# Attention weights turned by VectorE and DMA instead of TensorE, on one Trainium2 core

## Chip, core and metric

One core of a Trainium2 chip runs the kernel. The metric is the device time of one execution in microseconds (us). The kernel before took 1949.81 us, the median of 3 runs (1949.67 to 1951.08).

## What is computed

128 graphs of 128 nodes, width 512, 16 heads of 32, all in float32. `spatial_encoding` and `edge_encoding` are both `adj`, so the bias is `2 * adj`.

```python
q, k, v = (split_heads(x @ W.T) for W in (Wq, Wk, Wv))
a = einsum('bhnd,bhmd->bhnm', q, k) * 512 ** -0.5 + (adj + adj)[:, None]
row_nonzero = any(a != 0, axis=-1, keepdims=True)
p = softmax(where(row_nonzero, a, -inf)); p = where(isnan(p), 0, p)
o = einsum('bhnm,bhmd->bhnd', p, v)
out = layernorm(x + merge_heads(o) @ Wo.T)
```

## The kernel before, in words

Four graphs make a group (`GG`), 32 groups in all. Four heads make a tile, four tiles a group. One **round** `f` (the code says phase) handles one tile of one group: 4 graphs x 4 heads = 16 score blocks of 128 x 128. There are 128 rounds, `LAST` is the last. Every engine has its own instruction list, written out by hand, and the lists meet in semaphores.

Matrix products of weights (kinds k, q, v, o) are made as three float32r products of high and low parts, 12 matmuls of 512 columns a product, 16 products a group. `PLAN` deals them to the rounds: (kind, index, groups ahead). They go through three PSUM banks `ps_w` in turn, and `wait_bank` waits until the product three uses ago has been taken out of its bank.

A round on the engines:

- **PE** (`build`, tensor block): `turn(f-1, i)` transposes the 16 blocks of normalised weights of the round before (L468) into `ps_w` and `ps_o`; `scores(f)` (L481); `values(f-1)` (L495), which multiplies v by the turned weights `e_t` into `ps_o`; then the products of `slots(f)` (L396 to L407).
- **ACT**: takes products out of their banks (`take`, L573), copies turned weights from PSUM to `e_t` (`turned_out`), runs 16 exps with row sums (`exps`, L630) once `bias` has made the rows of a graph, writes the high part of the values (`values_hi`), normalises output rows (`normalise`, L616), and splits x chunks (`chunk_hi`).
- **DVE**: `add` (L757) and `moments` (L768, L770) for output rows, `bias` (L781, 16 instructions: minus scores minus doubled adj, with row minimum), `any_nonzero` (L791: maximum of 2048 elements a lane, so that with the minimum a row of zeros is found), `abs_largest` (L800, L805), and for each half (two graphs) `reciprocals` (L813) and `normalise` (L822 and L826, two instructions of 512 elements); `values_lo` (L719); `double_adj` (L729) once a group.
- **POOL**: low parts of x chunks (`chunk_lo`, L301) and the small operations of layernorm (`ln`, L324 to L339).
- **SP**: all loads and stores, by group.

`neg_a` (biased rows), `e_sb` (weights) and `e_t` (turned weights) each exist once: `bias(f)` waits for all exps of round f-1, and DVE runs `normalise` of the second half before the next `bias`.

Of the kernel before, what the change touches and what calls it, by code (L numbers as in the profile page):

```python
# [6 lines left out]
F32R = mybir.dt.float32r  # L7
ALU = mybir.AluOpType
# [12 lines left out]
GG = 4  # L21
# [3 lines left out]
BANKS = 3  # L25
SCALE = float(D) ** -0.5
# [9 lines left out]
PLAN = [[("k", 1, 0), ("q", 1, 0), ("v", 0, 1), ("v", 1, 1)],  # L36
# [3 lines left out]
FIRST_PLAN = [[("q", 1, 0), ("v", 0, 0), ("v", 1, 0), ("v", 2, 0), ("v", 3, 0)],  # L40
# [3 lines left out]
LAST_PLAN = [[("k", 1, 0), ("q", 1, 0), ("k", 2, 0)],  # L44
             [("q", 2, 0), ("k", 3, 0), ("o", 0, -1)],
             [("q", 3, 0), ("o", 1, -1)],
             [("o", 2, -1), ("o", 3, -1)]]
BEFORE = [("k", 0, 0), ("q", 0, 0), ("k", 1, 0)]
LAST = PHASES - 1
# [3 lines left out]
def slots(f):  # L53

    g, t = f // TILES, f % TILES
    if f < 0:
        plan, g = BEFORE, 0
    elif f == PHASES:
        plan = AFTER
    elif g == GROUPS - 1:  # L60
        plan = LAST_PLAN[t]
    else:
        plan = PLAN[t] if g else FIRST_PLAN[t]
    return [(kind, g + ahead, index) for kind, index, ahead in plan]
# [6 lines left out]
def bank_uses():  # L71

    uses = list(slots(-1))
    for f in range(PHASES):
        if f:
            uses += [("t", f - 1, i) for i in range(0 if f == LAST else 1, GG)]
        uses += slots(f)
    return uses + [use for use in slots(PHASES) if use[2] != 1]  # L80
# [10 lines left out]
def window_chunk(f):  # L91

    g, t = f // TILES, f % TILES
    chunk = {3: (g + 2, 1), 0: (g + 1, 3)}.get(t)
    return chunk if chunk and 2 <= chunk[0] < GROUPS and f < PHASES else None


def late_chunk(f):
    g, t = f // TILES, f % TILES
    chunk = {2: (g + 2, 0), 3: (g + 2, 2)}.get(t)  # L100
    return chunk if chunk and 2 <= chunk[0] < GROUPS and f < PHASES else None


def build(nc, xt_d, x_d, adj_d, wq_d, wk_d, wv_d, wo_d, out_d):
    ctx = ExitStack()
    with ctx:
# [6 lines left out]
        def sem(name):  # L113
# [14 lines left out]
        e_t = sb("e_t", [P, GG, TH, NODES])  # L128
# [6 lines left out]
        neg_min = sb("neg_min", [P, GG, TH])  # L135
        sums = sb("sums", [P, GG, TH])
        recip = sb("recip", [P, GG, TH])
        abs_max = sb("abs_max", [P, GG, TH])
# [12 lines left out]

        ps_w = [bank(f"ps_w{n}") for n in range(BANKS)]
# [11 lines left out]
        x_loaded = sem("x_loaded")  # L164
# [11 lines left out]
        biased = sem("biased")  # L176
        min_done = sem("min_done")
        exp_done = sem("exp_done")
        turned = sem("turned")
        turned_copied = sem("turned_copied")  # L180
        values_done = sem("values_done")
        abs_done = sem("abs_done")
# [12 lines left out]
        stored = sem("stored")  # L195
# [3 lines left out]
        xt_stage = {(g, c): buffer[:, c].rearrange("p a b -> p (a b)")  # L199
                    for g, buffer in ((0, neg_a), (1, e_t)) for c in range(CH)}  # L200
# [8 lines left out]
        def turned_bank(f, i):  # L209
            if f == LAST:  # L210
                return ps_s[(1, 2, 3, 1)[i]]
            return ps_w[USE["t", f, i] % BANKS] if ("t", f, i) in USE else ps_o
# [7 lines left out]
        def _(sp):  # L220
# [7 lines left out]
            def load_chunk(g, c):  # L228
                if g >= GROUPS:
                    return  # L230
                if g > 2 or c >= 2:
# [5 lines left out]
            def store(g, i):  # L237
                if g >= 0:
                    sp.wait_ge(normed, count("o", g, i))
                    sp.dma_start(out_d[g, :, i, :], x_row(g, i)).then_inc(stored, 16)  # L240

            def load_x(g):
                if g == 0:
                    sp.wait_ge(w_hi_done, 4 * CH)
                    sp.wait_ge(wo_lo_done, CH)
                else:
                    sp.wait_ge(stored, 16 * GG * g)
                sp.dma_start(x_sb[:, :, :], x_d[g]).then_inc(x_loaded, 16)
# [13 lines left out]
            for g in range(GROUPS):  # L262
                store(g - 2, 3)
                if g + 1 < GROUPS:
                    if g:
                        sp.wait_ge(biased, GG * TILES * g)
                    sp.dma_start(adj_sb[:, (g + 1) % PAIR], adj_d[g + 1]).then_inc(adj_loaded[(g + 1) % PAIR], 16)
                if g:
                    load_x(g - 1)
                load_chunk(g + 2, 0)  # L270
                load_chunk(g + 2, 1)
                if g == GROUPS - 1:
                    sp.wait_ge(values_done, GG * g)
                    sp.dma_start(v_sb[:, 1 - g % PAIR], x_d[g]).then_inc(last_x_loaded, 16)
                store(g - 1, 0)
                store(g - 1, 1)
                load_chunk(g + 2, 2)
                store(g - 1, 2)
                load_chunk(g + 2, 3)
            store(GROUPS - 2, 3)  # L280
            for i in range(GG):
                store(GROUPS - 1, i)
            sp.wait_ge(stored, 16 * GRAPHS)

        @block.gpsimd
        def _(pool):
# [13 lines left out]
            def rest(out, whole, hi):  # L300
                return pool.tensor_tensor(out, whole, hi.bitcast(F32), ALU.subtract)  # L301

# [76 lines left out]
            for f in range(PHASES):  # L379
# [544 lines left out]
```

## Time and profile before

| | |
|---|---|
| median of 3 runs | 1949.81 us |
| the profiled execution | 1949.59 us, its span 1947.8 us |
| TensorE busy | 1928.2 us (99%) |
| VectorE, ScalarE, GpSimd busy | 1475.5, 1490.9, 419.5 us |
| DMA | 116.41 MB, 60 GB/s |
| granted TensorE clock | 0.998 of full speed |

Busy time counts an engine's own instructions. It doesn't say what the engine would have had to wait for; that is read from the start times of a round in the timeline. The full clock is 2.4 GHz.

### The profile page before, as it was taken

The numbers are of one execution on the slowest core, as the hardware profiler recorded it, in microseconds if no ns is written. First come the engines' busy times: TensorE is split into PE (matmuls) and PEld (weight loads), VectorE is DVE, ScalarE is ACT, GpSimd is POOL, SyncE is SP. The second block draws the span as 40 slices with busy tenths as digits, with TensorE's granted clock in tenths as the row PEclk, the third lists the DMA queues.
The fourth block names the chain that finished last, engine by engine and source line by source line (L and its number), as shares of the span: only waits on it lengthen the run. The fifth ranks groups of instructions, "written<-read, shape, count | busy, mean of one in ns | idle before, by whom it ended". The sixth has DMA issues, their size and how long they took to land. (4 is left out here: it accounts for less than half of the span.)

```text
span 1947.8 us, 49249 instructions
## 1 busy us (share of the span) xinstructions
PE 1928.2 (99%) x16402; PEld 1607.4 (83%) x16402; DVE 1475.5 (76%) x6068; ACT 1490.9 (77%) x5394; POOL 419.5 (22%) x1268
## 2 busy tenths in 40 slices
PE   9999999999999999999999999999999999999997
PEld 7888888888888888888888888888888888888885
DVE  6787777778777887778777777877788777877776
ACT  7787778777777777788777877777777777877775
POOL 2122111222112221222211122211222122221102
PEclk9999999999999999999999999999999999999999
DMA  4121111211112201122111221112220112211111
GB/s 152 50 72 39 51 61 66 71 55 40 56 66 72 72 29 55 61 72 72 36 54 61 66 71 55 40 55 66 72 72 28 55 61 71 72 35 54 50 61 45
DMA packets 48637, 116.41 MB, mean 60 GB/s; under 512 B 5376, under 2 KB 5376, under 8 KB 44288
## 3 DMA queue, kind: packets, MB, share of 16 engines
q1 hardware_dynamic: 47808, 112.22, 17.0%
q8 instruction: 131, 2.15, 0.5%
q14 instruction: 122, 1.00, 0.2%
q10 hardware_dynamic: 576, 1.05, 0.2%
HBM read 79.69 MB, written 33.55 MB: 58 GB/s over the span
## 5 line engine op out<-in xcount | busy, mean ns | idle before, releaser
L630 ACT ACTIVATE e_sb<-neg_a,neg_max 128x128 f32<-128x128 f32 x2048 | 792.3, 391 | 93.5 <-DVE neg_max L781 93.2
L781 DVE CUSTOM_DVE_ANT_0 neg_a<-ps_s,adj_sb 128x128 f32<-128x128 f32 x2048 | 442.6, 286 | 369.1 <-PE ps_s L481 369.1
L404 PE MATMUL ps_w<-xt_hi,w_lo 128*128 128x512 f32 x1020 | 412.5, 404 | 0.0
L405 PE MATMUL ps_w<-xt_lo,w_hi 128*128 128x512 f32 x1020 | 398.4, 391 | 0.0
L630 ACT ACTIVATION_READ_ACCUMULATOR e_sb<-neg_a,neg_max 128x1 f32 x2048 | 388.1, 190 | 0.0
L826 DVE SCALAR_TENSOR_TENSOR e_sb<-e_sb,r_inv 128x512 f32<-128x512 f32 x512 | 331.0, 687 | 9.2 <-DVE r_inv L822 0.5
L791 DVE TENSOR_REDUCE neg_min<-neg_a 128x16 f32<-128x2048 f32 x129 | 292.7, 2269 | 4.4
L301 POOL TENSOR_TENSOR xt_lo<-xt_raw,xt_hi 128x512 fp32r<-128x512 f32 x120 | 155.6, 1297 | 576.9 <-ACT xt_hi L573 576.9
L407 PE MATMUL ps_w<-xt_hi,w_hi 128*128 128x512 f32 x1020 | 273.8, 390 | 0.0
L404 PEld LDWEIGHTS ps_w<-xt_hi,w_lo 128*128 128x128 f32 x1020 | 191.2, 187 | 62.3 <-issue 25.6
L573 ACT ACTIVATE e_t<-ps_o 128x512 f32<-128x512 f32 x126 | 75.2, 597 | 201.4 <-PE ps_o L468 201.4
L407 PEld LDWEIGHTS ps_w<-xt_hi,w_hi 128*128 128x128 f32 x1020 | 191.5, 188 | 42.3
L405 PEld LDWEIGHTS ps_w<-xt_lo,w_hi 128*128 128x128 f32 x1020 | 191.5, 188 | 36.4
L324 POOL TENSOR_TENSOR ln_tmp<-mean_var,constants 128x1 f32<-128x1 f32 x122 | 23.1, 190 | 858.8 <-DVE mean_var L770 854.1
L573 ACT ACTIVATE e_t<-ps_w 128x512 f32<-128x512 f32 x382 | 200.5, 606 | 1.4 <-PE ps_w L468 1.2
L404 PE MATMUL ps_w<-w_hi,xt_lo 128*128 128x512 f32 x512 | 199.2, 389 | 0.0
L405 PE MATMUL ps_w<-w_lo,xt_hi 128*128 128x512 f32 x512 | 199.2, 389 | 0.0
L404 PE MATMUL ps_w<-w_hi,o_lo 128*128 128x512 f32 x496 | 193.1, 389 | 0.0
L405 PE MATMUL ps_w<-w_lo,o_hi 128*128 128x512 f32 x496 | 193.0, 389 | 0.0
L468 PE MATMUL ps_w<-ident,e_sb 128*128 128x128 f32 x1528 | 188.1, 273 | 1.7 <-DVE e_sb L826 1.7
L573 ACT ACTIVATE v_sb<-ps_w 128x512 f32<-128x512 f32 x128 | 76.3, 596 | 137.0 <-PE ps_w L407 136.7
L468 PEld LDWEIGHTS ps_w<-ident,e_sb 128*128 128x128 f32 x1528 | 170.6, 140 | 2.4 <-issue 2.4
(105 smaller groups left out, 2838.9 us busy)
## 6 DMA issues: line engine op xcount, KB each, us to landing
x_sb<-x SPq DMA_DIRECT2D x31, 1024.0 KB, 4.8
out<-x_sb SPq DMA_DIRECT2D x124, 256.0 KB, 2.4
xt_raw<-xt SPq DMA_DIRECT2D x120, 256.0 KB, 2.8
adj_sb<-adj SPq DMA_DIRECT2D x32, 256.0 KB, 2.9
v_sb<-wk ACTq DMA_DIRECT2D x4, 256.0 KB, 6.3
neg_a<-xt SPq DMA_DIRECT2D x4, 256.0 KB, 5.8
e_sb<-wq SPq DMA_DIRECT2D x4, 256.0 KB, 7.7
v_sb<-wv SPq DMA_DIRECT2D x4, 256.0 KB, 8.3
```

The lines of the kernel that those rows point to most:

```text
L301: return pool.tensor_tensor(out, whole, hi.bitcast(F32), ALU.subtract)
L324: pool.tensor_tensor(ve, mean_var[:, i, 1:2], eps, ALU.add).then_inc(pool_step, 1)
L404: pe.matmul(out, lhs_lo(c), rhs_hi(c), start=(c == 0), stop=False)
L405: pe.matmul(out, lhs_hi(c), rhs_lo(c), start=False, stop=False)
L407: last = pe.matmul(out, lhs_hi(c), rhs_hi(c), start=False, stop=(c == chunks - 1))
L468: last = pe.transpose(turned_bank(f, i)[:, h * P:(h + 1) * P], e_sb[:, i, h, :], ident[:, :])
L573: return act.activation(out, in_, ACT.Copy, scale=scale)
L630: last = act.activation(e_sb[:, i, h, :], neg_a[:, i, h, :], ACT.Exp, scale=-1.0, bias=neg_max[:, i, h:h + 1], accum_out=sums[:, i, h:h + 1])
L781: last = dve.tensor_tensor_reduce(out=neg_a[:, i, h, :], in0=ps_s[h][:, i * NODES:(i + 1) * NODES], in1=adj_sb[:, g % PAIR, i, :], scale=- ...
L791: dve.tensor_reduce(neg_min[:, a:b].rearrange("p a b -> p (a b)"), neg_a[:, a:b].rearrange("p a b c -> p (a b) c"), AX.X, ALU.max).then_in ...
L826: dve.scalar_tensor_tensor(out=e_sb[:, i], in0=e_sb[:, i], scalar=BIG, in1=r_inv[:, i].unsqueeze(2).to_broadcast([P, TH, NODES]), op0=ALU. ...
```

## The change

- PE turns weights in the last round alone. In the others DVE transposes the 32 x 32 blocks of a half in one instruction (`turn_blocks`, from `e_sb` to a new buffer `e_b`), SP saves each half to DRAM (`save_blocks`, rows of 1 KB) and, once both are saved, loads them back with four DMAs, one for each 32 partitions, which puts the blocks in their places in `e_t` (`move_blocks`, rows of 2 KB).
- Values are made two rounds later than their scores: PE's round is `values(f-2)`, `scores(f)`, products.
- `PLAN` gives each round one k, one q, one v and one o product.
- `any_nonzero` no longer reads 2048 elements on DVE. POOL compares the biased rows of a half with zero into bytes, folds them as 32-bit integers three times (`zeros`), and DVE adds up the 16 bytes a row that are left and compares the sum with 128.
- `normalise` of a half is one instruction of 1024 elements. `bias` also waits until POOL has read the rows before.
- x rows are loaded by 256 KB instead of 1 MB; SP's list goes by rounds.
- `add` stands ahead of `bias`, `moments` and `values_lo` behind it; POOL's layernorm stands behind the zeros.

```diff
-PLAN = [[("k", 1, 0), ("q", 1, 0), ("v", 0, 1), ("v", 1, 1)],
-        [("k", 2, 0), ("q", 2, 0), ("o", 0, -1), ("o", 1, -1)],
-        [("k", 3, 0), ("q", 3, 0), ("o", 2, -1), ("o", 3, -1)],
-        [("k", 0, 1), ("q", 0, 1), ("v", 2, 1), ("v", 3, 1)]]
+PLAN = [[("k", 1, 0), ("q", 1, 0), ("v", 3, 0), ("o", 3, -2)],
+        [("k", 2, 0), ("q", 2, 0), ("v", 0, 1), ("o", 0, -1)],
+        [("k", 3, 0), ("q", 3, 0), ("v", 1, 1), ("o", 1, -1)],
+        [("k", 0, 1), ("q", 0, 1), ("v", 2, 1), ("o", 2, -1)]]
...
+            def save_blocks(f, half):
+                sp.wait_ge(transposed, 2 * f + half + 1)
+                sp.dma_start(blocks_d[f % 2, :, :, half], blocks_half[:, half]
+                             ).then_inc(saved[half], 16)
+
+            def move_blocks(f):
+
+                for half in range(2):
+                    sp.wait_ge(saved[half], 16 * (f + 1))
+                if f:
+                    sp.wait_ge(values_done, f)
                 else:
...
+                for b in range(BLOCKS):
+                    rows = slice(BLOCK * b, BLOCK * (b + 1))
+                    sp.dma_start(e_t[rows, :].rearrange("p (a c) -> p a c", a=BLOCKS),
+                                 blocks_d[f % 2, :, b].rearrange("(a j) m c -> j a (m c)", a=BLOCKS)
+                                 ).then_inc(moved, 16)
...
+            for f in range(PHASES):
+                g, t = f // TILES, f % TILES
+                if f:
+                    save_blocks(f - 1, 1)
+                store(f - O_LAG - 2)
+                load_x(f - GG)
+                load_chunk(loaded_chunk(f))
...
+                if f:
+                    move_blocks(f - 1)
...
+                if f < LAST:
+                    save_blocks(f, 0)
...
+            def zeros(f, half):
+
+
+                n = 2 * f + half
+                rows = neg_a[:, 2 * half:2 * half + 2].rearrange("p i h n -> p (i h n)")
+                pool.wait_ge(biased, GG * f + 2 * half + 2)
+                if n:
+                    pool.wait_ge(folded_done, n)
+                pool.tensor_scalar(is_zero[:, :].bitcast(U8), rows, 0.0, None, ALU.is_equal).then_inc(zero_step, 1)
+                words = is_zero[:, :].rearrange("p (r c) -> p r c", r=2 * TH)
+                pool.wait_ge(zero_step, 3 * n + 1)
+                pool.tensor_tensor(folded_once[:, :, :], words[:, :, 0:16], words[:, :, 16:32], ALU.add).then_inc(zero_step, 1)
...
             for f in range(PHASES):
+                chunk_lo(window_chunk(f))
+                zeros(f, 0)
+                zeros(f, 1)
                 if f:
                     ln(f - 1, -1)
...
+                if f:
                     pe.wait_ge(o_lo_done, f)
+                if f < LAST:
+                    pe.wait_ge(moved, 16 * BLOCKS * (f + 1))
...
             for f in range(LAST):
-                if f:
-                    for i in range(GG):
-                        turn(f - 1, i)
+                if f > 1:
+                    values(f - 2, range(GG), ps_o)
                 scores(f)
-                if f:
-                    values(f - 1, range(GG), ps_o)
...
+            def turn_blocks(f, half):
+                if f:
+                    dve.wait_ge(saved[half], 16 * f)
+                dve.wait_ge(normalised, 2 * f + half + 1)
+                dve.transpose(blocks[:, half],
+                              e_sb[:, 2 * half:2 * half + 2].rearrange("p i h (b j) -> p (i h) b j", b=BLOCKS)
+                              ).then_inc(transposed, 1)
...
+            for f in range(PHASES):
                 if f:
                     add(f - 1, -1)
+                bias(f)
+                if f:
                     moments(f - 1, -1)
-                if f % TILES == TILES - 1 and f + 1 < PHASES:
+                if f > 1:
+                    values_lo(f - 2)
+                if f % TILES == TILES - 1 and f < LAST:
                     double_adj(f // TILES + 1)
...
+                for half in range(2):
+                    any_nonzero(f, half)
+                    reciprocals(f, half)
+                    normalise(f, half)
+                    if f < LAST:
+                        turn_blocks(f, half)
+                    else:
+                        add(LAST, half)
```

## Rows read from the trace of the kernel before

**Rows 1.** The page, part 1: busy time, share, instructions of each engine.

```profile
PE 1928.2 (99%) x16402; PEld 1607.4 (83%) x16402; DVE 1475.5 (76%) x6068; ACT 1490.9 (77%) x5394; POOL 419.5 (22%) x1268
```

**Rows 2.** Timeline of PE, one round: start, duration, engine, line, operation.

```profile
929.09 0.60 PE L468 MATMUL ps_o<-ident,e_sb 128*128 128x128 f32 x4
...
930.92 1.17 PE L481 MATMUL ps_s<-k_sb,q_sb 32*128 32x128 f32 x32
932.03 1.08 PE L495 MATMUL ps_o<-e_t,v_sb 128*32 128x128 f32 x32
933.04 0.50 PE L404 MATMUL ps_w<-xt_hi,w_lo 128*128 128x512 f32 x1
...
944.07 0.60 PE L468 MATMUL ps_o<-ident,e_sb 128*128 128x128 f32 x4
```

**Rows 3.** Timeline of PE: the scores of rounds 4 and 124.

```profile
76.70 1.17 PE L481 MATMUL ps_s<-k_sb,q_sb 32*128 32x128 f32 x32
...
1875.08 1.17 PE L481 MATMUL ps_s<-k_sb,q_sb 32*128 32x128 f32 x32
```

**Rows 4.** Timeline of DVE, one round from its first bias.

```profile
932.16 0.29 DVE L781 CUSTOM_DVE_ANT_0 neg_a<-ps_s,adj_sb 128x128 f32<-128x128 f32 x1 [4.71 <-PE ps_s L481]
...
935.66 2.29 DVE L791 TENSOR_REDUCE neg_min<-neg_a 128x16 f32<-128x2048 f32 x1
...
938.05 0.18 DVE L800 SCALAR_TENSOR_TENSOR abs_max<-neg_max,neg_min 128x16 f32<-128x16 f32 x1
...
940.06 0.20 DVE L813 RECIPROCAL recip<-sums 128x8 f32<-128x8 f32 x1
...
941.76 0.68 DVE L719 TENSOR_TENSOR o_lo<-ps_o,o_hi 128x512 fp32r<-128x512 f32 x1
942.36 0.68 DVE L757 TENSOR_TENSOR x_sb<-ps_w,x_sb 128x512 f32<-128x512 f32 x1
943.07 0.70 DVE L768 BATCH_NORM_STATS2 ln_stats<-x_sb 128x6 f32<-128x512 f32 x1
943.80 0.18 DVE L770 BATCH_NORM_AGGREGATE mean_var<-ln_stats 128x2 f32<-128x6 f32 x1
```

**Rows 5.** Groups by form: shapes, count, busy us, mean ns, idle before.

```profile
L791 DVE TENSOR_REDUCE neg_min<-neg_a 128x16 f32<-128x2048 f32 x127 | 290.3, 2286 | 4.4
...
L791 DVE TENSOR_REDUCE neg_min<-neg_a 128x8 f32<-128x1024 f32 x2 | 2.4, 1209 | 0.0
```

**Rows 6.** Timeline of ACT: first and last of the 16 exps of that round.

```profile
933.19 0.40 ACT L630 ACTIVATE e_sb<-neg_a,neg_max 128x128 f32<-128x128 f32 x1 [1.35 <-DVE neg_max L781]
...
939.46 0.40 ACT L630 ACTIVATE e_sb<-neg_a,neg_max 128x128 f32<-128x128 f32 x1
```

**Rows 7.** Groups by form, POOL.

```profile
L301 POOL TENSOR_TENSOR xt_lo<-xt_raw,xt_hi 128x512 fp32r<-128x512 f32 x120 | 155.6, 1297 | 576.9 <-ACT xt_hi L573 576.9
...
L327 POOL TENSOR_TENSOR ln_tmp<-ln_tmp,constants 128x1 f32<-128x1 f32 x122 | 67.2, 551 | 0.0
...
L329 POOL TENSOR_TENSOR ln_tmp<-ln_tmp 128x1 f32<-128x1 f32 x122 | 23.6, 193 | 9.6
...
L296 POOL TENSOR_SCALAR_AFFINE_SELECT ident<-ident 128x128 f32<-128x128 f32 x1 | 0.3, 292 | 0.2 <-POOL two_constants L294 0.2
```

**Rows 8.** Timeline of DVE and POOL at 960.8.

```profile
960.81 0.39 DVE L729 TENSOR_SCALAR adj_sb<-adj_sb 128x512 f32<-128x512 f32 x1
960.84 0.41 POOL L335 TENSOR_TENSOR ln_tmp<-ln_tmp,constants 128x1 f32<-128x1 f32 x1
```

**Rows 9.** The page, parts 3 and 6: DMA queue, and us to landing.

```profile
q1 hardware_dynamic: 47808, 112.22, 17.0%
...
x_sb<-x SPq DMA_DIRECT2D x31, 1024.0 KB, 4.8
out<-x_sb SPq DMA_DIRECT2D x124, 256.0 KB, 2.4
```

**Rows 10.** Timeline of POOL: the four operations that split wo.

```profile
31.59 5.00 POOL L301 TENSOR_TENSOR w_lo<-x_sb,w_hi 128x512 fp32r<-128x512 f32 x4 [9.40 <-ACT w_hi L573]
```

More of the change, by code:

```diff
@@ L25 @@
 BANKS = 3
+BLOCK = 32
+BLOCKS = NODES // BLOCK
 SCALE = float(D) ** -0.5
@@ L63, in slots @@
         plan = PLAN[t] if g else FIRST_PLAN[t]
-    return [(kind, g + ahead, index) for kind, index, ahead in plan]
+    return [(kind, g + ahead, index) for kind, index, ahead in plan if g + ahead >= 0]
 def count(kind, g, index):
@@ L163, in build @@
         xt_loaded = [sem(f"xt_loaded{n}") for n in range(2)]
-        x_loaded = sem("x_loaded")
+        x_loaded = [sem(f"x_loaded{i}") for i in range(GG)]
         last_x_loaded = sem("last_x_loaded")
@@ L176, in build @@
         biased = sem("biased")
+        zero_step = sem("zero_step")
+        folded_done = sem("folded_done")
         min_done = sem("min_done")
         exp_done = sem("exp_done")
+        transposed = sem("transposed")
+        saved = [sem(f"saved{half}") for half in range(2)]
+        moved = sem("moved")
         turned = sem("turned")
@@ L668, in _ @@
             take(-1, 2)
-            for f in range(LAST):
-                n = len(slots(f))
-                if f:
-                    take(f - 1, -1)
-                    for i in range(GG):
-                        turned_out(f - 1, i)
-                    normalise(f - 1, -2)
+            for f in range(PHASES):
+                if f > 1:
+                    values_hi(f - 2)
                 chunk_hi(window_chunk(f))
@@ L680, in _ @@
                     exps(f, i)
[L681 to L688 removed]
+                    if i % 2:
+                        take(f, i // 2)
+                if f == 0:
+                    weight_hi("o")
+                else:
                     normalise(f - 1, -1)
                 chunk_hi(late_chunk(f))
[L691 to L700 removed]
+                for s in range(2, len(slots(f))):
+                    take(f, s)
             values_hi(LAST - 1)
[L702 to L705 removed]
+            turned_out(0)
+            turned_out(1)
             values_hi_half(0)
[L707 to L708 removed]
+            turned_out(2)
+            turned_out(3)
             values_hi_half(1)
[L710 removed]
             normalise(LAST, 0)
@@ L813, in reciprocals, with normalise @@
                 dve.reciprocal(recip[:, two], sums[:, two]).then_inc(recip_done, 1)
-            def normalise(f, half, nonzeros):
+            def normalise(f, half):
                 n = 2 * f + half
@@ L824, in normalise @@
                 dve.wait_ge(r_done, n + 1)
-                for i in range(2 * half, 2 * half + 2):
-                    dve.scalar_tensor_tensor(out=e_sb[:, i], in0=e_sb[:, i], scalar=BIG,
-                                             in1=r_inv[:, i].unsqueeze(2).to_broadcast([P, TH, NODES]),
-                                             op0=ALU.min, op1=ALU.mult).then_inc(normalised, 1)
+                dve.scalar_tensor_tensor(out=e_sb[:, two].rearrange("p i h n -> p (i h) n"),
+                                         in0=e_sb[:, two].rearrange("p i h n -> p (i h) n"), scalar=BIG,
+                                         in1=r_inv[:, two].rearrange("p i h -> p (i h)").unsqueeze(2
+                                         ).to_broadcast([P, 2 * TH, NODES]),
+                                         op0=ALU.min, op1=ALU.mult).then_inc(normalised, 1)
+            def turn_blocks(f, half):
+                if f:
+                    dve.wait_ge(saved[half], 16 * f)
[3 more added lines that the diff above has]
+                              ).then_inc(transposed, 1)
             for c in range(CH):
@@ L919 @@
     out = nc.dram_tensor("out", [GROUPS, NODES, GG, D], F32, kind="ExternalOutput").ap()
-    build(nc, *aps, out)
+    blocks = nc.dram_tensor("blocks", [2, P, BLOCKS, 2, 2 * TH * BLOCK], F32, kind="Internal").ap()
+    build(nc, *aps, out, blocks)
     r = run_bass_kernel_spmd(nc, [arrays], core_ids=[0])
```

309 lines of the change are left out of this document (121 added, 188 removed), and 4 rows, old and new, of the table FIRST_PLAN.

## The prediction

> **What bounds the kernel now.** I read the busy shares first: TensorE (PE) works 99% of the span [rows 1]. Next I laid one round of its timeline out by the start times of its four kinds of work [rows 2]: transposes 929.09 to 930.92, so 1.83 us; scores to 932.03, 1.11 us; values to 933.04, 1.01 us; the four weight products until the next transposes at 944.07, 11.03 us. The sum is 14.98 us and nothing in it is a wait. The starts of the scores of rounds 4 and 124 [rows 3] give (1875.08 - 76.70) / 120 = 14.99 us a round, so one round stands for all. The span of 1947.8 is then 76.7 before round 4, 1798.4 of rounds and 72.7 behind.
>
> **PE after the change.** The 16 transposes of a round go, in all rounds but the last: 13.15 us a round are left (1.01 + 1.11 + 11.03). The products are only dealt out differently, one of each kind to a round. That is the floor; the rest asks which engine or queue can't hold 13.15.
>
> **VectorE (DVE), term by term, start to start** [rows 4]. add 942.36 to 943.07: 0.71. bias 932.16 to 935.66: 3.50. moments: 0.73 and about 0.20. values_lo 941.76 to 942.36: 0.60. Doubling adj every fourth round: 0.10. These are 5.84 us. Each half then has a reduction of 128 bytes a lane, a compare, reciprocal, r_inv, normalise and the new transpose. Reciprocal to the end of normalise takes 940.06 to 941.76, 1.70, and the merged normalise costs the same. A tiny operation with a wait takes 0.28 (938.05 to the next). The byte reduction: the two reductions of rows 5 differ by 1.08 us for 1024 elements, which leaves about 0.27. The transpose of 1024 elements isn't in this trace. Its nearest row is the one-source reduction of 1024 elements, 1.209 us [rows 5], 1.15 in sequence. Below, the doubling of adj does 512 elements in 0.39 [rows 8], so 0.7 for 1024; above I allow half the reduction's pace, 2.2. I take 1.15: the row nearest in size, with one source and 4-byte elements. A half is 0.27 + 0.20 + 1.70 + 1.15 = 3.32 us, two are 6.65, and DVE needs 12.5 us a round. The removed reduction of 2048 elements (2.2 in sequence) pays for nearly all of the two transposes. So DVE has only 0.65 us to spare against PE.
>
> **ScalarE (ACT)** loses four copies and has 16 exps, from 933.19 with one copy between to the last at 939.46 [rows 6]: 6.7 us, with at most six other operations of 0.5 to 0.8. It fits in 13.15. In the chain it matters thus: bias starts at 0, the exps end at 7.7, and DVE reaches the second half at 5.1 + 3.3 = 8.4 anyway. Hidden, with 0.7 us of cover.
>
> **GpSimd (POOL)** gets per half a compare of 1024 elements and three folds of 128, 64 and 32 words. Its rows [rows 7]: a two-input operation takes 1.297 us at 512 elements and 0.193 at one, so 2.16 ns an element; the one-input select takes 0.292 at 128, so 0.8 to 1.5 ns an element, depending on how much of it is fixed. The folds by the two-input row: 0.47, 0.33, 0.26 and 0.3 of waits between, 1.4 us. The compare, P: 1.0 to 1.6 by the select, 2.4 by the two-input row. I take about 1.3, the one-input row being nearer in kind. A half costs 2.7. The first can start when two graphs are biased, 1.8, and is done at 4.5, before DVE asks at 5.1; the second at 7.2, before 8.4. POOL's whole round is 5.4 + 2.3 (layernorm) + 1.3 (a chunk) = 9.0 us. Hidden while P stays below about 1.6; the rival below says what lies above.
>
> A POOL operation of 0.19 us took 0.41 when it started 0.03 us behind DVE's doubling of adj, whose duration was unchanged [rows 8]: the later one waited. The Trainium skill (SBUF — State Buffer, Who interferes with whom) says that a DVE instruction with two SBUF inputs and a POOL instruction that reads SBUF exclude each other, whoever issued first. By that rule normalise may wait for a POOL fold, up to 0.47 a half; the rows allow nought to that. I charge 0.2 a half: DVE 12.9, still under 13.15. The skill's GPSIMD Engine Reference (4.1, Engine selection) calls one-input work on POOL roughly line-rate; an estimate by it would be P = 1.0 and the sum the same.
>
> **The queue of SyncE (SP) and DMA.** Each round adds two saves of 512 KB in 1 KB pieces and four moves of 256 KB in 2 KB pieces, six issues of about 0.4 us on SP, which has 13 us. Now q1 moves 112.22 MB in 17.0% of 16 engines [rows 9], 339 GB/s while busy. 2 MB more is 6.2 us of all engines a round, 7.5 if the short pieces cost half as much again; with today's 2.6 it is at most 10.1 of 13.15. Latency: 256 KB land in 2.4 us, 1 MB in 4.8 [rows 9]; a save about 3.2, then the moves at 4.8 plus 1.2 of issue, plus up to 2.3 behind the loads and stores that SP issues between: 9 to 12 us from the second transpose to the last move. Values wait for it. The second transpose ends 11.8 us after bias starts, and values of the next round but one begin 24.05 us after it: 12.2 us of cover. Saves wait for transposes and moves for saves, and behind them in SP's order stand the stores and x loads; those have a round to spare. What is late next, if the moves are: PE, by T = (14.15 + L) / 2, with L the latency.
>
> **Ends.** In round 0 the zeros stand on POOL behind the split of wo, 31.59 to 36.6 now [rows 10], some 3 us earlier after the change. Two halves of 2.7 end about 39, DVE's second half about 43, and bias of round 1 waits for it; today it isn't so. DVE and ACT then take some 11.2 us a round (no adds yet): bias of round 3 at 65, q of round 4 at 73, its scores at 74, against 76.70. All gain of the first rounds but 3 us is lost. At the end rounds 125 and 126 have three products and go by DVE's 12.5; the last values wait for a move, but turns remain on PE as now: 71 us against 72.7.
>
> **Sum.** 74 + 120 x 13.15 + 71 = 1723 us of span. The profiled execution took 1949.59 at a span of 1947.8, and the median is 1949.81, so 2 to 3 more: **1726 us**.
>
> **Rivals.**
> *A, the forecast: PE keeps the bound*, rounds of 13.1 to 13.3 us, 1715 to 1750. For it: all floors above lie below PE's. Against: three of them by less than 1 us. 45%.
> *B, POOL sets the pace through DVE.* If P is long, the compare of the second half is running when normalise of the first wants to start, and must end first: at 3.25 + 2P after bias. Then normalise, folds behind it, transpose, the second half and add make the round 10.0 + 2P. It decides from P = 1.6. At 2.0 it is 14.0 us and 1828 us. At 2.4, the two-input row, 14.8 and 1925. By the skill's rule of exclusion above, this is how it comes; without exclusion P = 2.4 makes the round only about 13.4 us (second half's zeros at 9.4, then 3.32 and 0.71). 26%, between 1750 and 1930.
> *C, the moves come late.* With L = 14 (the four moves get in each other's way, each filling only 32 partitions), T = 14.1 us, 1838 us. For it: it is the longest chain in the change and its row is an interpolation. 13%; 1750 to 1850.
> *D, the transpose goes at half pace*: DVE 12.5 + 2.1 = 14.6 us, 1900 us. Nothing in the trace speaks for it. 8%.
> *E, slower than before: B beyond its rows.* Place and mechanism as in B; from P = 2.5 us a compare to bytes (2.3 ns an element, over the two-input row) the round passes 14.98. At P = 2.8 it is 15.6 us, 2020 us. For it: POOL's power operation took 0.551 at one element against 0.193 of a multiply [rows 7], so operations differ. Against: one input. 6%. It would be the same time by C with L over 15.8.
> That the change does nothing is excluded: the transposes leave PE. Within 0.2%: 2%.
>
> **Range and chances.** Below: a start and an end 10 us better, 13.1 a round: 1708. Above, 1880 takes in C and two thirds of B, and leaves about 2 in 10 out. About 0.2% is what can be told from no change. Faster 0.92, same 0.02, slower 0.06.
>
> **What would show it.** PE's round by the starts of the scores: 13.15 (A). DVE's idle time before bias, on PE's scores, small but there (A), gone (B, D). The duration of POOL's compare against 1.6, and of normalise against 1.22 in one piece. The transpose at 1.2 or 2.3. The wait of values: on DMA only in C. Bias of round 1 at about 43. The forecast is wrong if the scores are over 13.4 us apart; the engine that never waits then names the rival.

## Result and the profile after

The changed kernel takes **2044.11 us** (median of 4 runs, 2042.71 to 2047.55), the kernel before 1949.76: a ratio of 1.0485 [1.0467, 1.0503]. It is slower by 4.9%; the forecast was 1726 us. The profiled execution took 2047.55 at a span of 2045.7.

The page of the changed kernel, parts 1, 3 and 4 (busy time; DMA queue; the chain that ended last, by line):

```profile
PE 1801.1 (88%) x14370; PEld 1452.7 (71%) x14370; DVE 1605.2 (78%) x6191; ACT 1228.8 (60%) x4886; POOL 1509.2 (74%) x2292
...
q1 hardware_dynamic: 268464, 378.61, 69.5%
...
POOL is_zero L357 24%; DMA e_t<-blocks 15%; DVE neg_a L822 6%; POOL folded_once L360 4%; POOL xt_lo L347 4%; DVE e_sb L860 4%; DMA blocks<-e_b 3%; PE ps_s L535 3%; PE ps_o L553 3%; POOL folded_twice L362 3%; SPq L292 2%; POOL folded L367 2%; POOL ln_tmp L398 2%; DVE e_b L870 2%; DVE x_sb L798 1%
```

PE works 127 us less than in [rows 1], but it is busy 88% of a longer span. The transposes that left it were 1.83 us in 127 rounds, 232 us; it works longer on the rest, which section 3 of the experiments comes back to. GpSimd (POOL) went from 22% to 74%, and its compare leads the chain. The groups (out<-in, shapes, count | busy us, mean ns | idle before, releaser) give the new operations' durations:

```profile
L357 POOL TENSOR_SCALAR is_zero<-neg_a 128x1024 uint8<-128x1024 f32 x256 | 711.0, 2777 | 158.6 <-DVE neg_max L822 137.5 <-POOL folded L367 20.8
L398 POOL TENSOR_TENSOR ln_tmp<-ln_tmp 128x1 f32<-128x1 f32 x122 | 141.3, 1158 | 9.6
L360 POOL TENSOR_TENSOR folded_once<-is_zero 128x128 int32<-128x128 int32 x256 | 117.8, 460 | 21.4
...
L870 DVE STREAM_TRANSPOSE e_b<-e_sb 128x1024 f32<-128x1024 f32 x254 | 316.3, 1245 | 27.0 <-DVE e_sb L860 0.5
L860 DVE SCALAR_TENSOR_TENSOR e_sb<-e_sb,r_inv 128x1024 f32<-128x1024 f32 x256 | 313.7, 1225 | 9.1 <-DVE r_inv L857 0.4
```

The compare takes 2.78 us where the forecast used 1.3; the transpose (1.245) and normalise (1.225) are as forecast. The landing times of the page, part 6, stand against those of [rows 9]:

```profile
blocks<-e_b SPq DMA_DIRECT2D x254, 512.0 KB, 3.3
e_t<-blocks SPq DMA_DIRECT2D x508, 256.0 KB, 6.3
x_sb<-x SPq DMA_DIRECT2D x124, 256.0 KB, 5.3
```

The waits of the changed kernel (total us, times, longest) say who stood where:

```profile
ACT x_sb L676 <- POOL shift L406: 703.8, 122, 6.4
...
DVE all_zero L835 <- POOL folded L367: 250.3, 253, 14.5
...
PE ps_o L553 <- DMA e_t<-blocks: 214.1, 90, 5.7
```

ScalarE (ACT) waits 5.8 us in every round for POOL's layernorm. That wait stands in no step of the forecast. Scores start at 85.84 in round 4 and at 1961.6 in round 124, so a round is 15.63 us against 14.99 [rows 3]; before round 4 lie 85.8 us and behind round 124 84.1. Rounds are no longer alike: 13.2 to 19.8 us between the starts of their scores.

One round of DVE and POOL, where the compare and the wait for it can be seen:

```profile
906.98 0.29 DVE L835 TENSOR_REDUCE all_zero<-folded 128x8 f32<-128x128 uint8 x1 [2.33 <-POOL folded L367]
907.37 0.73 DVE L839 TENSOR_SCALAR nonzero<-all_zero 128x8 f32<-128x8 f32 x1
...
908.49 1.22 DVE L860 SCALAR_TENSOR_TENSOR e_sb<-e_sb,r_inv 128x1024 f32<-128x1024 f32 x1
...
911.62 0.17 DVE L839 TENSOR_SCALAR nonzero<-all_zero 128x8 f32<-128x8 f32 x1
...
912.59 1.23 DVE L860 SCALAR_TENSOR_TENSOR e_sb<-e_sb,r_inv 128x1024 f32<-128x1024 f32 x1
...
915.10 0.65 DVE L798 TENSOR_TENSOR x_sb<-ps_w,x_sb 128x512 f32<-128x512 f32 x1
```

```profile
902.75 2.79 POOL L357 TENSOR_SCALAR is_zero<-neg_a 128x1024 uint8<-128x1024 f32 x1
...
907.03 2.77 POOL L357 TENSOR_SCALAR is_zero<-neg_a 128x1024 uint8<-128x1024 f32 x1 [0.16 <-POOL folded L367]
...
912.56 0.19 POOL L400 TENSOR_TENSOR ln_tmp<-ln_tmp,constants 128x1 f32<-128x1 f32 x1
912.83 1.04 POOL L402 TENSOR_TENSOR ln_tmp<-ln_tmp,constants 128x1 f32<-128x1 f32 x1
```

The first normalise (908.49 to 909.71) runs inside POOL's second compare (907.03 to 909.80), and neither is longer than elsewhere. The other way round it isn't so: a layernorm operation of 0.19 us that starts while the second normalise is running takes 1.04, until that normalise has ended. A third thing shows here: the tiny `tensor_scalar` of L839 takes 0.73 us inside the compare and 0.17 outside. It is so in all rounds: the median is 0.73 for the 128 that start inside a compare, 0.17 for the 128 others.

The profile thus names two suspects, POOL's compare (which is the forecast's rival E, 2020 us) and the moves of the blocks (its rival C). The experiments separate them.

### The profile page after: what moved, and what is told of

Its sections match the earlier page's. It is cut to its first block, busy times and chain, and to the rows that moved or that the text cites. A ratio compares the mean times of both kernels' runs of the same rounds, so it can differ in the third digit from the quotient of the medians.

```text
span 2045.7 us, 46740 instructions
## 1 busy us (share of the span) xinstructions
PE 1801.1 (88%) x14370; PEld 1452.7 (71%) x14370; DVE 1605.2 (78%) x6191; ACT 1228.8 (60%) x4886; POOL 1509.2 (74%) x2292
## 3 DMA queue, kind: packets, MB, share of 16 engines
q1 hardware_dynamic: 268464, 378.61, 69.5%
## 4 chain that ended last, share of the span: by engine, by line
POOL 43%; DMA 19%; DVE 15%; issue 10%; PE 7%; SPq 3%; ACT 1%; DVEq 0%; POOLq 0%; ACTq 0%
POOL is_zero L357 24%; DMA e_t<-blocks 15%; DVE neg_a L822 6%; POOL folded_once L360 4%; POOL xt_lo L347 4%; DVE e_sb L860 4%; DMA blocks<-e_b 3%; PE ps_s L535 3%; PE ps_o L553 3%; POOL folded_twice L362 3%; SPq L292 2%; POOL folded L367 2%; POOL ln_tmp L398 2%; DVE e_b L870 2%; DVE x_sb L798 1%
## 5 line engine op out<-in xcount | busy, mean ns | idle before, releaser
L357 POOL TENSOR_SCALAR is_zero<-neg_a 128x1024 uint8<-128x1024 f32 x256 | 711.0, 2777 | 158.6 <-DVE neg_max L822 137.5
L676 ACT ACTIVATE x_sb<-x_sb,shift,rstd 128x512 f32<-128x512 f32 x124 | 100.9, 815 | 708.0 <-POOL shift L406 703.8
L471 PE MATMUL ps_w<-xt_hi,w_lo 128*128 128x512 f32 x1020 | 426.6, 418 | 0.0
L472 PE MATMUL ps_w<-xt_lo,w_hi 128*128 128x512 f32 x1020 | 407.2, 399 | 0.0
L553 PE MATMUL ps_o<-e_t,v_sb 128*32 128x128 f32 x4080 | 167.3, 314 | 214.1 <-DMA e_t<-blocks 214.1
L870 DVE STREAM_TRANSPOSE e_b<-e_sb 128x1024 f32<-128x1024 f32 x254 | 316.3, 1245 | 27.0 <-DVE e_sb L860 0.5
L860 DVE SCALAR_TENSOR_TENSOR e_sb<-e_sb,r_inv 128x1024 f32<-128x1024 f32 x256 | 313.7, 1225 | 9.1 <-DVE r_inv L857 0.4
L553 PEld LDWEIGHTS ps_o<-e_t,v_sb 128*32 128x32 f32 x4080 | 128.0, 124 | 262.8 <-issue 261.2
L835 DVE TENSOR_REDUCE all_zero<-folded 128x8 f32<-128x128 uint8 x256 | 73.2, 286 | 250.3 <-POOL folded L367 250.3
L535 PE MATMUL ps_s<-k_sb,q_sb 32*128 32x128 f32 x4096 | 188.7, 333 | 0.0
```

Of the source, the lines that this page charges most:

```text
L357: pool.tensor_scalar(is_zero[:, :].bitcast(U8), rows, 0.0, None, ALU.is_equal).then_inc(zero_step, 1)
L471: pe.matmul(out, lhs_lo(c), rhs_hi(c), start=(c == 0), stop=False)
L472: pe.matmul(out, lhs_hi(c), rhs_lo(c), start=False, stop=False)
L535: last = pe.matmul(ps_s[h][:, nodes], q_sb[rows, slot, nodes], k_sb[rows, slot, nodes], start=True, stop=True)
L553: last = pe.matmul(out[HD * h:HD * (h + 1), i * P:(i + 1) * P], v_sb[:, g % PAIR, i, cols], weights, start=True, stop=True)
L676: act.activation(row, row, ACT.Identity, scale=rstd[:, i:i + 1], bias=shift[:, i:i + 1]).then_inc(normed, 1)
```

## Experiments

**1. Each suspect alone, and both.** In `e1` POOL compares 128 of the 1024 elements, in `e2` the saves and moves are gone, `e3` has both edits.

```diff
-  pool.tensor_scalar(is_zero[:, :].bitcast(U8), rows, 0.0, None, ALU.is_equal)
+  pool.tensor_scalar(is_zero[:, 0:32].bitcast(U8), rows[:, 0:128], 0.0, None, ALU.is_equal)   # e1, e3
-  save_blocks(f - 1, 1); move_blocks(f - 1); save_blocks(f, 0)          # e2, e3, with the waits on them
```

> The changed kernel, but POOL compares only 128 of the 1024 elements of a half with zero (the search for rows of zeros is left out for the rest). P falls from the measured 2.78 us to about 0.5. Theory POOL (the compare paces DVE, a round is 10.0 + 2P): PE's floor of 13.15 us a round, 1726 us in all. Theory MOVES (the second transpose to the values takes Q + L + 2.25 over two rounds, with L = 13.4 us in the changed kernel's trace): Q falls to 11.9 with the compare, a round is 13.8 us, 1815 us. If MOVES alone mattered and the compare did nothing: 2044 us still.

> The changed kernel without the saves and moves of weights: values multiply what happens to stand in e_t (the placing of turned weights is left out). Theory POOL: 10.0 + 2 x 2.78 = 15.6 us a round remain, about 2020 us. Theory MOVES: the wait is gone, 13.15 us a round, 1726 us.

> The short compare and no saves or moves together (both left out as in the two runs before). If the forecast's floors of PE and DVE were right and only these two terms wrong: 13.1 to 13.3 us a round, 1715 to 1750 us. If something else holds the round (DVE's own work, the order of lists, TensorE's clock): above 1760 us.

In `e2` and `e3` the values are made from what happens to stand in `e_t`, so their output is not the right one; they serve for the time alone.

Measured: `e1` **1822.94 us** (ratio 0.935 [0.9323, 0.9377]), `e2` **2011.24** (1.0316 [1.0286, 1.0346]), `e3` **1738.51** (0.8917 [0.8891, 0.8943]). Without its compare the change wins 221 us, without the moves 33, without both 306. POOL alone holds the changed kernel over the time of before; behind it stand the moves, worth 84 us once POOL is short (1823 to 1739). The rounds: 13.87 us in `e1`, 15.35 in `e2`, 13.24 in `e3`. The last is the forecast's PE floor of 13.15, so the floors of PE and DVE were right (PE is 98% busy there). The compare takes 0.538 us at 128 elements and 2.777 at 1024: 2.5 ns an element and 0.22 us fixed.

**2. The moves first on SP's list.** In `e4` SP issues the second save and the moves ahead of the round's store and loads instead of behind them; the output is the same. `e6` is this with the short compare of `e1`.

```diff
 save_blocks(f - 1, 1)
+move_blocks(f - 1)
 store(f - O_LAG - 2); load_x(f - GG); load_chunk(loaded_chunk(f))
-move_blocks(f - 1)
```

> The changed kernel with SP's moves of turned weights ahead of its store and its loads of x, chunk and adj instead of behind them. L should fall from 13.4 to about 10 us. Theory POOL: the round stays at 15.6, 2020 to 2044 us. Theory MOVES: (14.5 + 10 + 2.25) / 2 = 13.4 us a round, about 1765 us.

> The short compare (128 of 1024 elements, the rest of the search for zeros left out) and the moves ahead of SP's loads and stores, together. Q = 12.0 and L = 10.9 us, both measured apart, give (12.0 + 10.9 + 2.25) / 2 = 12.6 us by MOVES, under PE's 13.24 measured without any DMA: about 1740 us, as without saves and moves (1738.5). If the DMA's traffic itself costs, not its place in SP's list: near the 1823 of the short compare alone.

Measured: `e4` **2013.26 us** (1.0326 [1.0296, 1.0356]), `e6` **1754.97** (0.900 [0.8982, 0.9018]). `e4` is 7 under the range of theory POOL, `e6` 15 over its forecast of 1740. In `e4` the move of 256 KB lands in 4.9 us instead of 6.3, and the time from the second transpose to the values falls from 13.4 to 10.9 us. With the full compare this is worth what removing the moves was worth (2013 against 2011): it was their lateness that cost. With the short compare 16 us remain (`e6` 1755 against `e3` 1738.5), and there PE still waits for moves, 20 times, 19 us in all. SP's issues in both kernels (start, duration with what it waits for inside) show why:

```profile
911.09 4.62 SPq L279 DMA_DIRECT2D blocks<-e_b  x2
915.76 0.63 SPq L264 DMA_DIRECT2D out<-x_sb  x1
916.43 0.95 SPq L275 DMA_DIRECT2D x_sb<-x  x1
917.48 0.61 SPq L258 DMA_DIRECT2D xt_raw<-xt  x1
918.66 2.66 SPq L292 DMA_DIRECT2D e_t<-blocks  x4
```

```profile
912.17 4.25 SPq L279 DMA_DIRECT2D blocks<-e_b  x2
919.34 1.76 SPq L292 DMA_DIRECT2D e_t<-blocks  x4
921.15 0.43 SPq L264 DMA_DIRECT2D out<-x_sb  x1
```

Above is the changed kernel, below `e4`. In both the moves are issued about 3 us behind the last save, which they have to wait for; the three issues between fit into that wait. What differs comes after: with 0.75 MB of store and loads under way a move lands 1.4 us later (6.3 against 4.9, the medians). The round shown above also has slow issues, 2.66 us for four; that isn't the rule, as the median over rounds 6 to 119 is 1.75 us in the changed kernel and 1.76 in `e4`, and over 2 us are 29 of 114 rounds there and 7 here. So the cost is the traffic beside the moves rather than SP's queue. That is read from the traces; no run took the store and loads away.

**3. A lower clock of PE behind long stalls.** PE's timeline of the changed kernel, round at 914:

```profile
914.03 1.93 PE L553 MATMUL ps_o<-e_t,v_sb 128*32 128x128 f32 x32 [5.02 <-DMA e_t<-blocks]
915.89 2.09 PE L535 MATMUL ps_s<-k_sb,q_sb 32*128 32x128 f32 x32
...
929.13 1.08 PE L553 MATMUL ps_o<-e_t,v_sb 128*32 128x128 f32 x32
930.15 1.17 PE L535 MATMUL ps_s<-k_sb,q_sb 32*128 32x128 f32 x32
```

The busy time of the engines in stretches of this round (from:to, us, PE, PEld, DVE, ACT, POOL with their counts, PE's granted clock, DMA share, GB/s):

```profile
914.00:918.00 4.00, 3.97 (x65) 3.39 (x65) 1.75 (x2) 2.41 (x4) 0.78 (x3) 0.50 0.43 145
...
929.00:932.00 3.00, 3.00 (x68) 2.45 (x68) 2.77 (x5) 0.23 (x1) 2.27 (x7) 1.00 0.52 175
```

After 5.02 us without work PE is granted 0.50 of full speed, its level of 1.2 GHz, and values and scores take nearly twice the time of the round behind, 1.8 us more. Of 256 such groups 82 are over 1.5 us in the changed kernel (mean granted clock 0.942), 8 in `e4` (0.990), and 1 in `e9` below (0.997). Together they take some 60 us more PE time than in `e4`. How much of this lies on the path wasn't measured apart: `e4` took away stalls and low clock together, for 31 us. `e2` shows that a lower clock need not cost anything: its two executions had mean granted clocks of 0.964 and 0.947 and took 2011.23 and 2011.24 us, and PE worked 1806 us in the profiled one where `e4`, with 1760, took 2013. There another engine sets the round.

**4. What the round of `e4` is made of.** Once the moves are early, rounds are 15.35 us, and PE, with 13.15 of work, waits. ACT and POOL in `e4`:

```profile
900.17 0.81 ACT L675 ACTIVATE x_sb<-x_sb,shift,rstd 128x512 f32<-128x512 f32 x1 [5.93 <-POOL shift L405]
...
901.85 0.63 ACT L632 ACTIVATE xt_hi<-xt_raw 128x512 fp32r<-128x512 f32 x1
...
915.69 0.82 ACT L675 ACTIVATE x_sb<-x_sb,shift,rstd 128x512 f32<-128x512 f32 x1 [6.03 <-POOL shift L405]
...
930.10 0.82 ACT L675 ACTIVATE x_sb<-x_sb,shift,rstd 128x512 f32<-128x512 f32 x1 [5.46 <-POOL shift L405]
```

```profile
902.55 1.30 POOL L346 TENSOR_TENSOR xt_lo<-xt_raw,xt_hi 128x512 fp32r<-128x512 f32 x1 [2.42 <-ACT xt_hi L632]
903.82 2.79 POOL L356 TENSOR_SCALAR is_zero<-neg_a 128x1024 uint8<-128x1024 f32 x1
...
912.16 0.19 POOL L390 TENSOR_TENSOR ln_tmp<-mean_var,constants 128x1 f32<-128x1 f32 x1
...
915.46 0.19 POOL L405 TENSOR_TENSOR shift<-ln_tmp,rstd 128x1 f32<-128x1 f32 x1
...
918.23 2.79 POOL L356 TENSOR_SCALAR is_zero<-neg_a 128x1024 uint8<-128x1024 f32 x1 [2.57 <-DVE neg_max L821]
...
931.52 1.30 POOL L346 TENSOR_TENSOR xt_lo<-xt_raw,xt_hi 128x512 fp32r<-128x512 f32 x1 [1.45 <-ACT xt_hi L632]
933.00 1.30 POOL L346 TENSOR_TENSOR xt_lo<-xt_raw,xt_hi 128x512 fp32r<-128x512 f32 x1 [0.18 <-ACT xt_hi L632]
```

This is a closed circle over two in-order lists. ACT's normalise waits for POOL's layernorm. Behind it ACT makes the high part of the x chunk (from 900.17 to 902.55: 2.38 us), POOL waits for that to make the low part (1.27), and behind this stand both halves of zeros (8.34) and the next layernorm (3.49, of which about 1 is the operation held up by DVE's normalise). The sum is 15.5, and 915.69 - 900.17 = 15.52. In the one round of four without such a chunk, zeros wait for DVE's bias instead (918.23), and the circle through DVE is 930.10 - 915.69 = 14.41. One of the three others has two chunks: ACT makes a second high part on the way, and POOL's second low part starts at 933.00, so that normalise to normalise is 16.05. Two of 15.52, one of 16.05 and one of 14.41 make 15.38, and 15.35 was measured. `e10` is `e4` with the chunk's low part moved behind the layernorm:

```diff
-chunk_lo(window_chunk(f))
 zeros(f, 0); zeros(f, 1)
 if f: ln(f - 1, -1)
+chunk_lo(window_chunk(f))
```

> The kernel of e4_moves_first with one line of GpSimd's order changed: the low part of the window chunk (1.3 us, three rounds in four) stands behind the layernorm instead of ahead of the zeros; nothing is left out. Theory CIRCLE (read in e4's trace): a round there is the closed chain GpSimd layernorm -> ScalarE normalise 0.72, copy of v 0.48, high part of o 0.48, high part of the chunk 0.70 -> GpSimd chunk 1.27, zeros of both halves 8.34, layernorm 3.49 = 15.5 us, in the three rounds with a chunk, and 14.4 us in the fourth, where the zeros wait for VectorE's bias instead. With the chunk out of the chain all four rounds are 14.3 to 14.5 us, so 2011 - 120 x 1.0 = about 1890 (1880 to 1905). Theory POOL LOAD: GpSimd's busy time a round is what counts, in whatever order; it doesn't change, so 2005 to 2015.

Measured: **2215.47 us** (1.1362 [1.1329, 1.1395]), a miss. Three rounds of four were indeed shorter (bias to bias 14.4, 14.4 and 14.75 us), but the fourth took about 24.7. PE in that round:

```profile
933.91 0.76 PE L470 MATMUL ps_w<-w_hi,xt_lo 128*128 128x512 f32 x1 [11.28 <-issue]
934.47 0.63 PE L471 MATMUL ps_w<-w_lo,xt_hi 128*128 128x512 f32 x1
```

The product of v needs the low part that POOL has just finished (932.54 to 933.80 in its timeline): the chunk of the rounds with f % 4 = 1 is the last of the next group's, and that group's first product stands in the same round. I had moved it past its due time. (These matmuls, 0.63 us against 0.39 a few us later, are again slow after 11.28 us of idleness, at a granted clock of 0.58.) `e12` leaves this one chunk ahead of the zeros and moves the others.

> As e10_chunk_last, but the chunk of the rounds with f % 4 = 1 keeps its place ahead of the zeros: it is the last of the next group's, and that group's first product of v stands in the same round (in e10 three rounds of four were 14.4 us, as CIRCLE says, and the one with this chunk was 24.6, with PE waiting for its low part). Nothing is left out. Theory CIRCLE: three rounds of 14.4 and one of 15.5 make 14.7, so 2011 - 120 x 0.65 = 1933 (1920 to 1945). If the circle isn't what bounds e4: 2000 or more.

Measured: **1945.08 us** (0.9975 [0.9963, 0.9986]), 12 over the centre and at the edge of what was expected. Bias to bias the four rounds are 14.44, 15.50, 14.42 and 14.79 us: the round that kept its chunk is the long one. POOL works as much as in `e4` (1512 us, 1509 there) and 68 us are gone, so it was the place in the circle and not POOL's load. The changed kernel with two reorderings and nothing else is thus 0.25% faster than the kernel before, and no more: at least 14.4 us a round remain, with the two compares in them.

**5. From which compare does it bind?** `e7` is `e6` with 512 elements compared.

> As the run before, with 512 of 1024 elements compared (the rest left out). The two measured prices, 0.53 us at 128 and 2.77 at 1024, give P = 1.49. By the prediction's rival B the knee is at P = 1.6: 13.24 us a round, about 1740 us. If POOL's two halves in a row with its other work already pace DVE (zeros of the second half at 1.8 + 2 x (P + 1.45) = 7.7 after bias, 8.9 where a chunk stands before them, against 8.6 when DVE is there): up to 13.6 us in three rounds of four, up to 1780 us.

Measured: **1772.64 us** (0.9091 [0.9073, 0.9109]), the upper of the two. The compare took 1.499 us, the round 13.44, against 13.31 at 0.54 us. Without its two compares the circle of `e4` is 15.52 - 2 x 2.78 = 9.96, so 9.96 + 2 x 1.5 = 12.96 would be just below PE's 13.15. But in `e7` the second half's first fold starts inside DVE's normalise (910.07 to 911.30), in all 128 rounds, and takes 1.01 us instead of 0.46:

```profile
907.62 0.46 POOL L360 TENSOR_TENSOR folded_once<-is_zero 128x128 int32<-128x128 int32 x1
...
910.61 1.01 POOL L360 TENSOR_TENSOR folded_once<-is_zero 128x128 int32<-128x128 int32 x1
```

With that the circle is 13.5, over PE's round, and so it is from ACT's normalise to the next (902.39 to 915.91). So the compare binds a little below the threshold of 1.6 us that the forecast gave; that this was about right has a reason other than the one it gave.

**6. Is it the form of the compare?** `e8` is the kernel before with two unused operations a round on POOL, in four forms by turns.

```diff
+form = f % 4   # 0: is_equal to bytes, 1: is_equal to float32, 2: mult by 1, 3: subtract of two halves, 512 elements
+look(f, 0); look(f, 1)          # ahead of the layernorm ln(f, -2); bias of round f waits for the looks of round f - 1
```

> The kernel before, with two operations a round added on POOL whose outputs nobody uses, over 1024 elements of the biased rows: by round in turn a compare to bytes, a compare to float32, a multiply to float32, and a subtraction of two halves (two inputs, 512 elements). If compares or byte outputs are what is dear: 2.77 us for the first, near 1 us for the multiply. If a one-input operation costs 2.5 ns an element in any form: 2.77 for the first three, 1.3 for the last. Theory EXCLUSION (POOL reading SBUF and DVE's two-input normalise shut each other out): normalise durations up to 1.5 us over their 0.69 where a compare is running; without exclusion 0.68 to 0.70 all through. The time stays within 0.3% of before in either case, as DVE has 2 us to spare.

Measured: **2096.86 us** (1.0754 [1.0732, 1.0775]); that it would cost nothing was wrong. The forms themselves:

```profile
L320 POOL TENSOR_SCALAR words_out<-neg_a 128x1024 f32<-128x1024 f32 x64 | 178.2, 2784 | 5.8 <-POOL words_out L320 5.0 <-DVE neg_max L806 0.9
L316 POOL TENSOR_SCALAR bytes_out<-neg_a 128x1024 uint8<-128x1024 f32 x64 | 178.0, 2781 | 40.8 <-DVE neg_max L806 35.6 <-POOL bytes_out L316 5.2
L318 POOL TENSOR_SCALAR words_out<-neg_a 128x1024 f32<-128x1024 f32 x64 | 177.5, 2773 | 291.3 <-DVE neg_max L806 286.1 <-POOL words_out L318 5.3
...
L322 POOL TENSOR_TENSOR words_out<-neg_a 128x512 f32<-128x512 f32 x64 | 81.5, 1273 | 4.6
```

Neither the byte output nor the compare is to blame: a multiplication to float32 takes the same 2.78 us. And one input is dearer than two, not cheaper. With one input the three sizes 128, 512 and 1024 took 0.538, 1.499 and 2.777 us (`e1`, `e7`, the changed kernel), 2.5 ns an element at either step. With two, 512 took 1.273, and the folds of 128 and 32 words 0.460 and 0.251, 2.1 to 2.2 ns an element.

Where did `e8` lose 147 us? Three rounds of four stayed at 15.0 to 15.3 us, the fourth took 19.2 on average. I tried the order (`e11`: the looks behind the last layernorm) and the waits (`e13`: the looks read a weight that never changes, wait for nothing, and nobody waits for them).

> The kernel of e8_forms (the kernel before, with two operations a round over neg_a on GpSimd that nothing uses) with these two operations behind the round's last layernorm instead of ahead of it; nothing is left out. In e8 three rounds of four stayed at 14.98 us and one took 19.4. Theory ORDER: what was late there were the two layernorms of that round, queued behind 5.6 us of unused work; behind them the same work costs little: 1950 to 1975. Theory LOAD (GpSimd's reads of SBUF slow VectorE or hold it off, or 5.6 us more of GpSimd are too much in the round that also has two layernorms of 2.6 us and two chunks of 1.3): again 2050 to 2100.

> The kernel of e8_forms with its two unused GpSimd operations a round reading a weight that stays in place instead of neg_a: they wait for nothing but each other, and no engine waits for them; place and forms are as in e8 (5.6 us a round in three rounds of four, 2.7 in the fourth). Nothing is left out. Theory WAITS: what cost 145 us in e8 and 310 in e11 were the waits tied to these operations (the layernorms and VectorE's bias stood behind them, and they behind bias); without them GpSimd has 15 us a round for some 9 of work: 1950 to 1965. Theory LOAD: SBUF reads of GpSimd or its full queue cost by themselves: 2050 or more.

Measured: `e11` **2261.17 us** (1.1597 [1.1563, 1.163]), `e13` **2095.0** (1.0745 [1.0714, 1.0776]). Neither of the theories that hoped for 1950 to 1975 holds; `e11` is over the range of its other theory too (2050 to 2100), `e13` is in its. In `e11` two rounds of four took 19.8 us: now the looks stood behind layernorms that come late in the round, and the next bias behind the looks (473 us of DVE's waits in `e11` are for them). `e13` is the plain case. Its waits:

```profile
ACT x_sb L640 <- POOL shift L361: 140.2, 29, 4.9
```

29 times, once a group, ACT's normalise waits 4.9 us for a layernorm that stands behind 5.6 us of unused work on POOL; the exps stand behind that normalise on ACT's list, DVE's reciprocals behind the exps, PE's transposes behind DVE. 140 us is nearly all of the 145 that `e13` lost. DVE's normalise kept its 0.69 us in `e8`, so POOL's reads didn't slow it. (The doubling of adj, a `tensor_scalar`, did get longer beside the unused work: 0.73 us in `e8` and `e13`, 0.39 in the kernel before; it comes once a group.) This is the same link from POOL to ACT as in the changed kernel, seen in the kernel before. It is read from the waits; no run put the unused work behind that one layernorm alone.

**7. Without the compare.** `e9` has the moves first and no zeros on POOL. DVE finds a row of zeros from two numbers a row that are there anyway: the row's largest score is 0 and its exps add up to 128.

```diff
-dve.tensor_reduce(all_zero[:, half], folded[:, half].bitcast(U8), AX.X, ALU.add)
-dve.tensor_scalar(nonzero, all_zero, 128.0, None, ALU.not_equal)
+dve.tensor_scalar(differs[:, half], sums, 128.0, None, ALU.not_equal)
+dve.scalar_tensor_tensor(out=nonzero, in0=neg_max, scalar=0.0, in1=differs[:, half], op0=ALU.not_equal, op1=ALU.max)
```

> The changed kernel with the moves first and no zeros on POOL: DVE tells a row of zeros by its row maximum being 0 and its sum of exps being exactly 128 (this differs from the reference for a row whose values are not all 0 but within float32 rounding of it). Theory POOL + MOVES: nothing is late, 13.24 us a round, first rounds faster as POOL's zeros no longer stand behind the split of wo: 1725 to 1740 us. If DVE's own work sets the round: it has 12.65 - 0.4 us, no change.

Measured (median of 4 executions): **1740.39 us** (0.8926 [0.8911, 0.8941]), 10.7% under the kernel before. The page:

```profile
PE 1709.3 (98%) x14370; PEld 1379.5 (79%) x14370; DVE 1485.6 (85%) x6191; ACT 1236.7 (71%) x4886; POOL 539.6 (31%) x1268
```

Rounds are 13.28 us and PE is the bound again, as the forecast had it for the whole change. A row whose nonzero scores are too small for its exps to differ from 1 would be taken for zeros. The given inputs hardly tell the two tests apart: the diagonal of `adj` is at least 0.05, so a row of zeros isn't to be expected in them.

## Why the prediction was wrong

**PE after the change: right.** Forecast 13.15 us a round, 13.24 in `e3` and 13.28 in `e9`. Even where PE isn't the bound, its work is that.

**DVE: right.** Forecast 12.5 (12.9 with 0.2 a half for waits); in `e3` a round from the first bias to the end of add takes 12.3 us, and 12.7 in the one of four with the doubling of adj. The transpose, which no row showed, was taken at 1.15 in sequence and is 1.245 long, 1.17 in sequence.

**GpSimd: the step that failed, twice.** First the size. P was taken at 1.3, "the one-input row being nearer in kind"; it is 2.77. The row chosen was a select of 128 elements; the row set aside, two inputs at 2.16 ns an element [rows 7], was the nearer one in size and gave 2.4. The small row couldn't tell fixed time from time per element, and the choice took one input to be cheaper, which `e8` shows to be the wrong way round. Even the upper bound was too low for that reason: the two-input slope of 2.16 ns was right for two-input operations, and one-input ones have 2.5. The folds, from the same two-input row, were 0.47, 0.33 and 0.26 in the forecast and 0.460, 0.321 and 0.251 in the trace. The Trainium skill (GPSIMD Engine Reference, 4.1 Engine selection) calls one-input work on POOL roughly line-rate; the sentence on it gave P = 1.0, and the trace disagrees by nearly three times. Rival E, the compare over its rows, had 6%, and its sum at P = 2.8 was 15.6 us a round and 2020 us. `e2` and `e4` have 15.35 us a round, and 2011 and 2013 us.

Second the mechanism. Rivals B and E let normalise wait for the compare. The rows above exclude that: normalise runs inside the compare, 1.22 us as elsewhere. The Trainium skill (SBUF — State Buffer, Who interferes with whom) states that such a pair exclude each other whoever came first; the trace agrees in one direction only, a layernorm operation that starts inside normalise taking 1.04 instead of 0.19. By the forecast's other formula, without exclusion, P = 2.8 gives 1.8 + 2 x (2.8 + 1.4) + 3.32 + 0.71 = 14.2 us, which is nearly the circle through DVE (14.4 measured). What makes 15.5 of it is the circle through ACT. The forecast had added up POOL's busy time, 9.0 us, and called it hidden; it named who waits for the zeros but not what stands behind them on POOL's list (the layernorm), nor what stands behind that on ACT's. That 10.0 + 2P and the measured 9.96 + 2P agree is chance.

**DMA: mechanism right, size off.** 9 to 12 us were forecast from the second transpose to the last move; the median is 12.6, with the moves landing in 6.3 instead of 4.8. To the start of the values, which PE isn't always free to take up at once, it is 13.4. The formula T = (14.15 + L) / 2 gives 13.77 for 13.4, and `e1`, where only the moves are late and it is 13.4 too, has 13.87. The part that was mis-sized is traffic beside the moves; the 3 us of the save were right (3.3). The share of the queue, 69.5% at a longer round and 77.0% in `e1`, corresponds to 10.7 to 10.9 us a round, over the 10.1 that were called the most (half as much again on the 1 MB of saves makes 7.7, not 7.5, and 10.3 in all). Rival C (1838 us) would have come with a short compare: `e1` is 1823.

**Ends: late for the same reason.** Bias of round 1 starts at 45.3 (forecast 43), scores of round 4 at 85.8 (74) and the tail is 84.1 (71). Both zeros halves of round 0 pass POOL behind the split of wo. In `e9`, without them, bias of round 1 is at 31.8 and scores of round 4 at 68.2.

The sum by terms: start +12, 120 rounds at 15.63 instead of 13.15 +298, tail +13, which are the 323 us between the spans, 1723 and 2046. In whole kernels: the compare alone is worth 221 us (`e1`), the moves alone 33 (`e2`), and another 52 come only when both are gone (`e3`), since each hides part of the other; `e3` is 12 over the forecast.

**What stays open.** What the lower clock alone cost in the changed kernel, and why a tiny `tensor_scalar` of DVE (L839, 8 elements) takes 0.73 us while POOL compares 1024 elements and 0.17 otherwise. It goes with the compare (0.30 inside one of 512 elements in `e7`), and the forecast's 0.20 for it held outside alone; which of the two engines' accesses get in each other's way isn't shown.

## What to carry to other kernels

An operation moved to another engine is not hidden because that engine is idle 78% of the time: list what stands behind it on that engine's in-order list, who waits for that, and what stands behind that wait, until the chain closes, and compare the length of the circle with the round. Price an operation that the trace doesn't show by the row nearest in size, not by the one that looks alike but is eight times smaller, and if the threshold lies between two rows, give the worse one its weight. A reordering needs the due time of each thing it moves (`e10`), and the cheapest version of a test may be one that reads numbers already made (`e9`).

## What the hardware did that was not expected

- A one-input operation on POOL costs 2.5 ns an element and 0.2 us fixed, 2.78 us at 1024, to bytes or to float32, compare or multiply; at 512 elements it took 1.50 us (`e7`), the two-input one 1.27 (`e8`).
- DVE's normalise (one tensor and one broadcast input) isn't held up by a POOL compare in progress (1.22 us inside and outside), but a POOL operation of 0.19 us that starts inside it takes 1.04 to 1.17, and a fold of 0.46 took 1.01 (`e7`). A DVE `tensor_scalar` of 8 elements took 0.73 us inside such a compare, 0.17 outside.
- DVE's transpose of 32 x 32 float32 blocks takes 1.245 us for 1024 elements a lane.
- With 0.75 MB of stores and loads issued just before them, the moves of 256 KB landed in 6.3 us; issued ahead of these, in 4.9 (medians).
- After 5.02 us without work PE's values and scores took 1.93 and 2.09 us instead of 1.08 and 1.17, at a granted clock of 0.50.
